# T5 layers of a vision tower on one core: key projections ahead of query projections, earlier turns, and a dense layer's first up products inside the attention before it

## What is computed

```
nx = t5_layer_norm(h, ln1[i])
q, k, v = nx @ attn_q[i], nx @ attn_k[i], nx @ attn_v[i]     # 12 heads of 64
attn = softmax(q k^T + bias)
h = h + (attn v) @ attn_o[i]
nx = t5_layer_norm(h, ln2[i])
y = relu(nx @ ffn_wi[i]) @ ffn_wo[i]
if i in (1, 3): y = y + moe_ffn(nx)                          # 8 experts, best 2
h = h + y
```

## Time and profile before

| what | us |
|---|---|
| three runs | 1831.17, 1829.98, 1817.59 (median 1829.98) |
| profiled execution | 1824.8, its span 1823.0 |
| TensorE busy | 1551.9 (85% of the span) |
| VectorE busy | 960.6 (53%) |
| ScalarE busy | 833.8 (46%) |
| GpSimd busy | 525.7 (29%) |

### The profile page before, as it was taken

The page is one execution under the profiler, slowest core; times in us unless marked ns, Lnnn a source line. Parts: engine busy times, 40 slices in busy tenths (PEclk is TensorE's granted clock), DMA queues, the critical chain, the costliest instruction groups (busy, mean ns, idle before and its releaser), DMA issues.

```text
span 1823.0 us, 33509 instructions
## 1 busy us (share of the span) xinstructions
PE 1551.9 (85%) x11921; PEld 1424.4 (78%) x11921; DVE 960.6 (53%) x2758; ACT 833.8 (46%) x2100; POOL 525.7 (29%) x1259
## 2 busy tenths in 40 slices
PE   5898997895789898989987999789989998889980
PEld 5788776894678787888877999678878887889980
DVE  4665556332654566445665444356654667534426
ACT  1544531442555565356533555345643555245531
POOL 2246335005522022532332000544245123300021
PEclk8866755895767899899988999879989999899995
DMA  4120101452069100100004677400020000257731
GB/s 144 31 80 11 45 18 40 135 168 62 26 216 282 37 1 19 49 19 1 17 21 132 200 221 214 125 16 2 1 66 18 1 11 22 61 180 221 229 95 38
DMA packets 87753, 149.20 MB, mean 82 GB/s; under 512 B 7380, under 2 KB 58995, under 8 KB 87590
## 3 DMA queue, kind: packets, MB, share of 16 engines
q1 hardware_dynamic: 81254, 134.81, 24.2%
q0 software_dynamic: 6336, 12.26, 2.4%
HBM read 106.05 MB, written 41.05 MB: 81 GB/s over the span
## 4 chain that ended last, share of the span: by engine, by line
PE 48%; issue 26%; DVE 12%; ACT 8%; POOL 4%; DMA 1%; another core or an unknown queue 1%; SPq 0%; DVEq 0%; POOLq 0%; ACTq 0%
PE ps_score L1276 9%; PE ps_proj L1259 7%; PE ps_proj L1081 6%; PE ps_proj L1205 5%; PE ps_proj L1095 4%; PE ps_score L1132 3%; PE ps_o L1170 3%; ACT qk L1340 3%; PE ps_score L1144 2%; PE ps_o L1180 2%; PE ps_proj L1062 1%; PE ps_turn L1016 1%; ACT probt L1404 1%; PE ps_pt L1041 1%; ACT qk L1295 1%
## 5 line engine op out<-in xcount | busy, mean ns | idle before, releaser
L1276 PE MATMUL ps_score<-w,hid 128*112 128x192 f32 (+2 forms) x1680 | 305.4, 334 | 8.6 <-issue 5.4
L1276 PEld LDWEIGHTS ps_score<-w,hid 128*112 128x112 f32 (+2 forms) x1680 | 277.4, 180 | 10.5 <-issue 6.5
L1415 ACT ACTIVATE hid<-ps_proj 128x224 f32<-128x224 f32 (+2 forms) x360 | 137.8, 385 | 271.2 <-PE ps_proj L1259 267.9
L1490 POOL DMA_INDIRECT tin<-rows_out,idx x66 | 66.5, 1008 | 469.1 <-issue 366.8
L1532 POOL TENSOR_SCALAR tmp<-rs,var 111x1 f32<-111x1 f32 x110 | 42.0, 382 | 549.0 <-DVE rs L1603 548.6
L1205 PE MATMUL ps_proj<-wo,ot 128*111 128x192 f32 (+1 forms) x616 | 143.6, 384 | 13.9 <-ACT ot L1379 10.3
L1303 ACT ACTIVATE xa_hi<-ps_turn,gainf 128x111 fp32r<-128x111 f32 x132 | 46.7, 354 | 216.9 <-PE ps_turn L1016 199.2
L1205 PEld LDWEIGHTS ps_proj<-wo,ot 128*111 128x111 f32 (+1 forms) x616 | 117.2, 208 | 27.6 <-issue 23.0
L1340 ACT ACTIVATE qk<-ps_proj,hscale 128x333 f32<-128x333 f32 (+1 forms) x192 | 89.7, 527 | 79.3 <-PE ps_proj L1081 78.5
L1144 PE MATMUL ps_score<-qk 128*74 128x37 f32 x1584 | 123.2, 238 | 1.7 <-ACT qk L1333 1.7
L1144 PEld LDWEIGHTS ps_score<-qk 128*74 128x74 f32 x1584 | 118.8, 151 | 5.1 <-issue 2.5
(11 more groups left out here) (255 smaller groups left out, 4181.9 us busy)
## 6 DMA issues: line engine op xcount, KB each, us to landing
w_in<-w_all_dram SPq DMA_DIRECT2D x130, 384.0 KB
w<-w_all_dram SPq DMA_DIRECT2D x50, 576.0 KB, 4.8
rows_in<-zero SPq DMA_DIRECT2D x1, 12320.0 KB, 46.1
rows_out<-zero SPq DMA_DIRECT2D x1, 9240.0 KB, 79.6
tin<-rows_in SPq DMA_DIRECT2D x36, 224.0 KB
rows_out<-tout SPq DMA_DIRECT2D x36, 168.0 KB
patch<-patches_dram SPq DMA_DIRECT2D x11, 333.0 KB, 2.9
wo<-wo_all_dram SPq DMA_DIRECT2D x6, 576.0 KB, 3.9
```

What stands on the lines that cost most here:

```text
L1276: last = pe.matmul(bank[0:n, 0:C], hid[:, i % 2, m, at:at + n], w2[:, slot, m, :], start=(m == 0), stop=(m == FC - 1))
L1415: act.activation(hid[:, i % 2, m, 0:n], bank[:, 0:n], ACT.Relu if b.tile is None else ACT.Gelu).then_inc(taken, 1)
L1490: pool.indirect_dma_start(gat[:, 2 * (n % GAT_RING) + k, :], None, src, bass.IndirectOffsetOnAxis(idx[:, g, k:k + 1], 0), bounds_check=DIS ...
```

## The change

```diff
--- before.py
+++ after.py
@@ -69,7 +69,7 @@
         self.blocks = DIAG_BLOCKS if a == DIAG else BLOCKS
         self.block_of = [b for b, (g0, n) in enumerate(self.blocks) for _ in range(n)]
         self.qk = 2 * self.chunks
-        self.qk_order = [c + 6 * k for c in range(6) for k in range(2)] if self.t5 else list(range(4))
+        self.qk_order = [c + 6 * k for c in range(6) for k in (1, 0)] if self.t5 else list(range(4))
         self.vparts = 2 if self.t5 else 1
         self.vwide = H * self.d // self.vparts
         self.pairs = 2
@@ -175,6 +175,9 @@
 TURN_AT_LATE = {(5, 2): 0, (5, 5): 1, (6, 2): 2, (8, 2): 3, (8, 5): 4, (9, 2): 5, (9, 5): 6, (10, 5): 7}
 LOGIT_AT = {(5, 2): 0, (5, 5): 1, (6, 2): 2, (8, 2): 3, (8, 5): 4, (9, 2): 5, (10, 2): 6}
 COUNT_AT = {(5, 5): 0, (6, 2): 1, (6, 5): 2, (8, 5): 3, (9, 2): 4, (9, 5): 5}
+UP_AHEAD = {-1: (0,), 0: (1,), 1: (2, 3), 2: (4, 5)}
+UPS = sum(len(m) for m in UP_AHEAD.values())
+DENSE_TURNS = ((1, 0), (1, 2), (1, 4))
 LOGITS_AHEAD = {0: 9, 2: len(LOGIT_AT), 4: len(LOGIT_AT)}
 COUNTS_AHEAD = {0: 8, 2: len(COUNT_AT), 4: len(COUNT_AT)}
 
@@ -305,7 +308,7 @@
         i = g - BLOCKS[b][0]
         if b + 1 < NB:
             g0, n = BLOCKS[b + 1]
-            places = [(0, 5), (1, 2), (1, 5)] if late else [(0, 2), (0, 5), (1, 2)]
+            places = [(0, 5), (1, 2), (1, 5)] if late else [(0, 2), (0, 4), (1, 1)]
             for k, (at, slot) in enumerate(places[:n]):
                 if at == i:
                     slots[slot].append(("A", g0 + k))
@@ -361,6 +364,8 @@
         if n >= 3:
             out.append(("PV", *divmod(n - 3, 2)))
         out += slots[3 * p + 2]
+        if follower[1] not in SPARSE:
+            out += [("next", ("U", 0, m)) for m in UP_AHEAD.get(n - pairs, ())]
         if n < pairs:
             out += [("E", g, p), ("DIV", g, p)]
     last = ATTS[a].vparts - 1
@@ -375,12 +380,12 @@
 
     out = []
     before = []
-    turns = [("A", g) for g in range(G - 3, G)]
     for b in range(NB):
         for m in range(FC):
-            out.append(("U", b, m))
-            if turns and m != 1:
-                out.append(turns.pop(0))
+            if b or m >= UPS:
+                out.append(("U", b, m))
+            if (b, m) in DENSE_TURNS:
+                out.append(("A", G - 3 + DENSE_TURNS.index((b, m))))
             if m % 2 and before:
                 out.append(before.pop(0))
             if b == NB - 1 and m in (1, 2, 4):
@@ -1070,7 +1075,7 @@
                     bank = proj_bank(key)
                     if b == 0:
                         pe.wait_ge(w1_ready, r + 1)
-                    if j == 0:
+                    if j == s.qk_order[0]:
 
                         for x_g in range(g0, g0 + n):
                             pe.wait_ge(xt_ready, TURNED[(st, "A", x_g)] + 1)
```

## The result

The changed kernel took 1807.9 us (median of 20 runs, 1795.94 to 1883.12) where the kernel before took 1821.26 us beside it (1813.99 to 1835.23): ratio 0.9916, 95% interval 0.9893 to 0.9939. That is 13.4 us between the medians and 15.3 us by the ratio (11.1 to 19.5); forecast were 9.2 us. The forecast time of 1816.7 us is 8.8 us above the measured one: 4.6 us of that come from the starting value of 1825.9 us, where the 20 runs of the kernel before have 1821.26, and 4.2 us from the gain. The changed kernel was timed twice more, on other occasions: 0.9932 (0.9905 to 0.9959) and 0.9950 (0.9923 to 0.9977). The mean of the three is 0.9933, 12.2 us of 1821. The first measurement's profiled execution ran at a lowered clock (span 1881.3 us, mean granted clock 0.757), so the rows "after" are those of the changed kernel's second profile, with a span of 1811.0 us and a clock of 0.855.

What follows compares the result with a forecast made beforehand. TensorE, with 48% of the chain of waits plus 26% issue time, was taken as the bound. Up products -11.1, keys +1.3 and turns +0.6 sum to -9.2 us from 1825.9: 1816.7 us, range 1804 to 1831.

Steps and rivals of the forecast that it cites:

- Up products: Ends of the two T5 attentions followed by dense layers: six up products fill TensorE's pauses, 11.1 us gained together.
- the first place: Attention end after the first T5 layer, up to block 2's first up product: gain 7.1 us.
- the second place: Attention end after the third T5 layer: 24.9 us replace 28.92, gain 4.0 us.
- Keys ahead: Key projections before queries in four layers: 34 value waits stay, scores wait longer, 1.3 us slower.
- The third layer's score waits: Scores' first step of a block after a sparse FFN: 0.72 us wait grows by 0.5 us, three times.
- value waits that fall by more than 2 us: Sign that the forecast is wrong: value projections' waits for ScalarE were to stay at some 34.
- waits for `w_in` in the tail: Sign of a wrong forecast: weight-transfer waits in the attention's end, taken as 0, kept at 0 to 2.8 us per place.
- Turns: Sooner turns in three layers: +0.9 us in the first, -0.3 in the two others, +0.6 us in sum.
- (a): Rival: clock stays at 0.50 between group 9's and the last output projection in both layers, 1831 us; chance 0.10.
- (b): Rival: the fill only swaps waits in the tails, slow stretches stay as many, 1823 us; chance 0.20.
- (c): Rival: slow stretches at the other attentions' starts also vanish, about 10 us more, 1806 us; chance 0.13.
- (d): Rival: ScalarE reloads its function table between Relu and exponentials; no added load in the built order, no chance given.

Runs made afterwards that it cites:

- e3: Kernel before with only the up products and the turns of the two dense layers moved: 1817.1 us beside 1824.51.
- e4: The changed kernel run again, unaltered: 1812.25 us beside 1824.51 for the kernel before, ratio 0.9932.
- e6: Changed kernel without the sooner turns, so keys and up products only: ratio 0.9912 to the kernel before.
- e7: Changed kernel with the last projection pair of the third T5 layer's blocks query then key again: that layer's stretch 1.2 to 1.6 us shorter; no total given.
- e9: The changed kernel run again as yardstick in another session: 1796.84 us beside 1806.88 for the kernel before, ratio 0.9950.
- e1: Kernel before with only the order of T5 key and query projections changed: 1815.72 us beside 1824.51.
- e2: Kernel before with only the turns moved sooner: 1824.51 us beside 1824.51.
- e5: Changed kernel with all parts set back, giving the program of the kernel before: ratio 0.9985 to the kernel before.
- e12: Changed kernel with the third layer's last pair query then key, up products earlier and spread, sooner turns kept: 1792.81 us beside 1806.88 for the kernel before.
- e11: Changed kernel with the third layer's last pair query then key, up products earlier and spread, turns set back: 1788.23 us beside 1806.88 for the kernel before.

## Why the prediction was right, and where it was not

The total moved the forecast way and lies in the range. It is 3 us beyond the likeliest gain by the mean of three measurements, 4 to 6 us beyond by the first alone. That it came so close is partly luck: the up products brought 3.1 us less than forecast, the keys 5.1 us more and with the other sign, and the two misses offset each other.

**Up products: right in mechanism, 3 us too large.** Step by step against the timeline after, counted from U0: the group 9 projection was due after 3.99 us and came after 3.94; the last projection was due after 12.1 and came after 12.0. The pauses are 0.37 (0.55 forecast) and 0.97 us (1.1). What was mis-sized is block 1, worked out as 10.9 us: it takes 11.5 (743.20 to 754.71). Its first third, two products, a turn and a down product, takes 3.71 us (743.20 to 746.91) where I had 3.48 without a turn and 0.15 for it, and the second third takes 4.02, since its turn comes late (748.09, 1.18 us behind the product's start). That is 0.6 us in each place. The larger part of the miss is the starting value: the 32.03 us of the earlier trace rows held a slow projection that two of four executions don't have. The mean of the four is 30.1 us, and from there the first place gains 4.7 and not 7.1 us, the second 28.9 - 25.5 = 3.4 and not 4.0. By B and C, means of four kernels without and five with these up products (e3, e4, e6, e7, e9): 40.6 - 36.0 = 4.6, and 39.0 - 35.7 = 3.3. So 8 us where 11.1 stood. The like-for-like part is the 3.4 us of the second place, where no profile has a slow projection; what the first place has beyond that rests on a projection at the lower clock in two profiles out of four. That a single profile's slow stretch may not be there in the next run should have been in the sum; the third layer, in the same profile, said so.

**Keys ahead: the wrong sign.** The text said "the value projection starts 0.03 us later than now", and that 34 waits stay. The rows after have the value projection 4.19 us behind the start of the first of the four projections (655.35 to 659.54); before it was 4.29 (651.88 to 656.17). The step that failed is the time at which the query's scaling starts: 0.87 us behind the key's activation, it said. It is 0.78 (656.40 to 657.18), since the second product, directly behind the first, is done sooner than 0.87 us later. The timeline of the kernel before already had that 0.78, from 652.73 to 653.51. ScalarE's chain from there (0.86, 0.98 and 0.33 us) is as forecast, with no room in it, so the 0.09 us reach the value projection, whose pause is 0.31 instead of 0.40 us. In the first and second layers of e1 eight value projections wait 0.09 to 0.13 us less each, one more of 0.2 to 0.3 us is gone, and the wait of block 3's second pair is 0.1 and 0.65 us shorter. Small numbers, many times: A is 354.0 us on the mean of four kernels with the old order (before, e2, e3, e5) and 350.2 on the mean of nine with the new. That is 3.8 us less; the ranges, 352.7 to 355.5 and 348.2 to 353.8, touch. Some of it is the clock's: A holds 23.9 us at 0.50 on the mean of the four and 22.0 on that of the nine, worth about 1 us (an estimate: half of the difference, since the group 9 projection took 4.11 us at 0.50 and 2.15 us at 1.00). The cleanest sign is in blocks with no time at 0.50: the second blocks of the second and fourth layers, with three value waits each, take 40.7 to 40.8 us in all four profiles with the old order and 40.4 to 40.6 in all nine with the new. With D, which did not move, it makes about -3.8 where +1.3 was forecast. The third layer's score waits went as forecast, 0.72 to 1.16 us, three times; what was left out is that its value waits fall as well (from 2.4 to 1.6 us), so D stands still. The forecast's own list of what would prove it wrong had "value waits that fall by more than 2 us"; they fell by 4.7, so by its own sign this term is wrong. The other sign that came, waits for `w_in` in the tail (0.23 and 0.60 us), cost nothing, as the forecast had priced it.

**Turns: right in sum.** Forecast +0.9 us in the first layer and -0.3 in the two others. With the keys ahead the first layer's share of A is 115.2 to 115.4 us in six kernels with the turns and 114.4 to 114.7 in three without: +0.8. The two others together are 235.0 us on the mean with (232.9 to 238.5) and 235.6 without: too scattered to tell -0.3 from nothing. With the old order of the keys the first layer went the other way, 114.6 us in e2 against 115.4 to 115.9, but e2's first block had 6.8 us at 0.50 and those of all the others 10.2. The third block of that layer, at full clock throughout, grew by 0.4 us with the turns in either order: 36.5 to 36.9, and 36.1 to 36.5 or 36.6. The wait for the split moves from the projection to the turn, as the text had it.

**The sum** in these measures is -8 - 3.8 + 0 = -12 us, which is what the three ratios give. The split into parts rests on the stretches; the single ratios of e1 and e3 put it the other way round, 9 and 3.5 us, and their intervals just miss the stretches' values. Nor do the stretches hold everything: from block 2's first up product to the next layer's first scores the five kernels with these up products take 1.0 us less in the first place and 0.4 us less in the second than the four without, by the means.

**The rivals.** (a) The clock stays low in the tail: fell. The windows show 1.00 from 729.3 to 743.2. Pauses of 0.37 to 0.49 and of 0.97 us lie in that stretch at a clock of 1.00, in both layers of e3, e4, e6, e7 and e9. The sum counted the tail at full clock; that was my estimate, from the 108 us at 1.00 in the earlier trace rows, in which 17 value projections of the kernel before wait 9.4 us in all. What did go with a low clock (0.50) are the longer pauses of 1.46 and 2.03 us ahead of the output projection of group 8. But a long pause did not always go with one: in the old order a pause of 1.83 us stands ahead of the last transposes, and the projection behind it ran at 1.00 in six of eight cases (2.15 us in e5). What brings the clock down, no run shows. (b) Fill only swaps waits, slow stretches stay: fell. The pauses did swap as worked out, but the tails are about 25.5 us in all five of these profiles, while without the fill they vary between 28.9 and 32.0. (c) All slow stretches at block starts vanish: no. The first layer's is still there (603 to 613 at 0.50); those of the second and fourth layers are gone in some profiles with the sooner turns and not in others (see e6). (d) No table reload, as said: the traces before and after hold six table loads each, of 1.28 us, none of them in a tail.

## What to carry to other kernels

A saving of 0.1 us that comes back two dozen times is worth as much as one long pause (here 0.09 us at the value projection shown, 4.7 us less of such waits in all, beside a longest pause of 2.03 us in the tail); so take the start of a second, chained product from a row of a second product, and not from the length of a first. Before a slow stretch goes into the sum, look whether the same place in a sister stage of the same profile has it; and when two profiles of a stretch differ, compare their time at the lower clock before giving the difference to an edit. And a filler product is worth its place where the engine stands still for another engine's work (the pause of 1.83 us ahead of the last transposes fell to 0.37 us); moving an instruction that itself waits for the busy engine only changed which row the wait is printed in (e2: 3.7 us less ahead of projections, 5.8 us more ahead of turns).

## What the runs showed of the hardware

- The clock of one stretch of the same program differs from run to run: the projection of 12 matmuls at the end of attention 3 took 4.11 us before (at 0.50) and 2.15 us in the same program again (e5, at 1.00), with the same pauses directly around it (1.83 and 0.64 us). In these two executions TensorE's granted clock did not follow from the instructions alone.
- The output projection behind TensorE's pauses of 1.46 and 2.03 us ran at 0.50 (the windows' third row), while with pauses of up to 0.97 us in the tail the clock stayed at 1.00 (e3, e4, e6, e7 and e9). In e12's third layer, with pauses of 0.25, 1.45 and 0.30 us at this place, that projection ran at 1.00 and took 2.20 us; in e11, with nearly the same ones, 3.27 us at a mean clock of 0.67.
- A product of five matmuls of 336 columns directly behind another was done 0.78 us after it; the first one, behind scores, took 0.85 us from start to start (655.35, 656.20 and 656.98 in the changed kernel, 651.88, 652.73 and 653.51 before).
- The kernel before had medians of 1824.5, 1818.6 and 1806.9 us in three sessions on three chips, 1% apart: only ratios within a session compare.
- In the third T5 layer the length of D goes with the time at the lower clock: 34.2 us at 0.50 went with 129.9 and 130.1 us, 30.7 with 126.4 to 126.8, and 23.9 with 124.0 and 124.3 (the last two with e7's edit in them).
